# A graph network's first edge stage: selection matrices as the weights, edge values as the moving operand, and one product that adds two halves and turns them

## The reference, cut to what matters

```python
h = jnp.maximum(_layernorm(x, axis=-1), 0.0)
r = edge_index[1]                                   # dst, sorted
c1ij = jnp.concatenate([h[r], edge_attr_64], axis=1)
e = jax.nn.softplus(c1ij @ W1 + b1)                 # 128 values per edge
e = jax.nn.softplus(e @ W2 + b2)                    # 128 values per edge
out = e @ W3 + b3
agg = jax.ops.segment_sum(out, r, num_segments=12500)
x = x + h + agg
```

## Time and profile before

| what | value |
|---|---|
| median of 3 runs | 7407.81 us (7402.51 to 7408.39) |
| the profiled execution, its own time | 7408.24 us |
| its span (first to last instruction) | 7406.7 us |
| mean granted TensorE clock | 0.874 |
| PE busy over the span | 6552.2 us, 88% |
| DVE, POOL, ACT busy | 5031.9 us, 4983.3 us, 3071.1 us |
| the first edge stage, first to last `mm1` | 111.4 us to 1419.9 us |

### The profile page before, as it was taken

One profiled execution on the slowest core, in us unless ns is written; L12 is line 12 of the kernel. 1 busy time (PEld: TensorE's weight loads), 2 busy tenths in 40 slices (PEclk: granted clock), 3 DMA queues, 4 the chain that ended last, 5 costly groups with the idle time before them and its releaser, 6 DMA issues.

```text
span 7406.7 us, 164037 instructions
## 1 busy us (share of the span) xinstructions
PE 6552.2 (88%) x35087; PEld 3274.1 (44%) x35087; DVE 5031.9 (68%) x15478; ACT 3071.1 (41%) x4956; POOL 4983.3 (67%) x6107
## 2 busy tenths in 40 slices
PE   6999999966787777777869999999999989998998
PEld 4666666532333333333324444444444434443443
DVE  7777777657888888888856777777777743332232
ACT  4777777634555555555523333333333300000000
POOL 4544544347777777777757777777777657765776
PEclk9999999975656565666579999999999999998999
DMA  4333333242232323232322222222222266665775
GB/s 129 107 106 106 106 107 105 95 144 83 86 90 85 90 85 90 85 90 85 91 53 60 61 63 61 61 61 62 62 61 61 50 177 189 189 187 170 199 200 165
DMA packets 774396, 770.05 MB, mean 104 GB/s; under 512 B 242791, under 2 KB 585891, under 8 KB 774179
## 3 DMA queue, kind: packets, MB, share of 16 engines
q1 hardware_dynamic: 575923, 589.45, 25.5%
q0 software_dynamic: 147776, 160.99, 10.6%
q10 hardware_dynamic: 50544, 17.90, 1.0%
HBM read 581.31 MB, written 187.29 MB: 104 GB/s over the span
## 4 chain that ended last, share of the span: by engine, by line
PE 59%; POOL 18%; issue 9%; DVE 8%; SPq 3%; DMA 1%; ACT 1%; DVEq 1%; POOLq 0%; ACTq 0%
POOL zone L1051 15%; PE ps L2566 9%; PE ps L2406 9%; PE ps L2211 6%; PE ps L2193 5%; PE ps L2218 5%; PE ps L2571 4%; PE ps L2398 4%; POOL zone L1090 2%; PE ps L2425 2%; PE ps L2209 2%; PE ps L2391 2%; PE ps L2387 2%; PE ps L2416 1%; DVE zone L1368 1%
## 5 line engine op out<-in xcount | busy, mean ns | idle before, releaser
L1051 POOL DMA_INDIRECT zone<-tab_msg,zone x1664 | 1636.3, 983 | 520.0 <-issue 512.1
L1051 POOL DMA_INDIRECT zone<-tab_u,src_i x1664 | 1604.7, 964 | 562.2 <-issue 552.2
L1368 DVE TENSOR_TENSOR zone<-ps,zone 128x512 f32<-128x512 f32 x1664 | 1068.0, 686 | 452.4 <-PE ps L2398 332.8
L2020 ACT ACTIVATE zone<-ps 128x792 fp8e4<-128x792 f32 x1200 | 966.7, 829 | 881.0 <-PE ps L2370 861.8
L2370 PE MATMUL ps<-zone 128*128 128x396 bf16 x2400 | 933.5, 478 | 290.8 <-DVE zone L1654 156.2
L2193 PE MATMUL ps<-zone 128*128 128x64 f32 (+1 forms) x6656 | 831.2, 282 | 174.9 <-DMA zone<-tab_msg,zone 158.6
L1654 DVE TENSOR_SCALAR zone<-tT,zone 128x392 bf16<-128x392 f16 x2400 | 968.5, 404 | 0.0
L2406 PE MATMUL ps<-zone,w_bas 128*64 128x512 f32 x3328 | 900.0, 619 | 0.0
L2193 PEld LDWEIGHTS ps<-zone 128*128 128x128 f32 (+1 forms) x6656 | 754.1, 196 | 320.0 <-issue 272.9
L2566 PE MATMUL ps<-zone 128*128 128x512 fp8e4 x3332 | 845.1, 383 | 26.6 <-DMA zone<-adj 16.2
L1333 DVE SCALAR_TENSOR_TENSOR zone<-zone,ps 128x512 f32<-128x512 f32 x832 | 566.3, 686 | 274.9 <-ACT zone L1921 174.5
(11 more groups left out here) (320 smaller groups left out, 8792.8 us busy)
## 6 DMA issues: line engine op xcount, KB each, us to landing
zone<-adj SPq DMA_DIRECT2D x238, 768.0 KB
adj<-zone SPq DMA_DIRECT2D x150, 784.0 KB, 3.4
zone<-in_dst_row SPq DMA_DIRECT2D x832, 128.0 KB, 2.7
zone<-in_ea_T SPq DMA_DIRECT2D x416, 128.0 KB, 2.6
zone<-src_lin SPq DMA_DIRECT2D x2448, 0.5 KB
zone<-adj SPq DMA_DIRECT2D x34, 896.0 KB
tab_msg<-zone SPq DMA_DIRECT2D x104, 256.0 KB, 2.3
zone<-tab_msg,zone POOLq DMA_INDIRECT x1664
```

What stands on the lines that cost most here:

```text
L1051: nc.gpsimd.indirect_dma_start(out=gat(e, u)[:, k, :], out_offset=None, in_=table, in_offset=bass.IndirectOffsetOnAxis(ap=numbers[:, c * T ...
L1368: nc.vector.tensor_tensor(zed[:, b % SL, :], bank(2 + b % 2), inter[:, u % 2, b % 2, :], ALU.mult) \
L2020: nc.scalar.activation(staging[m][:, :, at_ * 2 * WN:(at_ + 1) * 2 * WN].rearrange("p b (w d) -> p w b d", w=2), pair_[:, :, 0:CX].rearran ...
```

## The change

The sum is made in two steps. First (`sum_rows_of`), the selection of each group is the weights (128 edges x 64 nodes) and `hid2` is the moving operand (128 columns). Groups 0 and 2 write to partitions 0 to 63 of a bank, groups 1 and 3 to partitions 64 to 127. The result is 64 nodes on the partitions, twice, with 128 values along the row. Two chunks share bank 4 or 5. Second, ACT copies the two chunks of a bank to SBUF in one instruction (`move_rows`, into `sum_rows`), and PE multiplies each with `two_eyes`, two identity matrices of 64 one above the other (`turn_rows`): this adds the two halves and turns the result back into 128 values x 64 nodes, in bank 6 or 7, from where DVE adds it to `acc` as before. DVE's addition moves from lag 7 to lag 9.

```diff
+        two_eyes = sb("two_eyes", [P128, D])
+        sum_rows = spare.rearrange("p (v s c) -> p v s c", v=2, s=2)
+            const(nc.gpsimd.tensor_tensor(two_eyes[:, :], ident[:, 0:D], ident[:, D:P128], ALU.add))
...
-            ADD_LAG = {0: 7, 1: 4, 2: 7}
+            ADD_LAG = {0: 9, 1: 4, 2: 7}
...
-                    dve.wait_ge(agg_done, done(ga, it, u, depth(e)))
+                    dve.wait_ge(rows_summed if e == 0 else agg_done, done(ga, it, u, depth(e)))
...
-                        (5, soft(hid2_ready, softened2, agg_done, soft2, hid2, 2)),
+                        (5, soft(hid2_ready, softened2, rows_summed, soft2, hid2, 2)),
                         (0, selT_stage(0, p, slice(D, P128), 3)),
                         (4, sel_stage(0, p)),
-                        (ADD_LAG[0], add_stage(0, p, H, (4, 5, 6, 7)))]
+                        (ADD_LAG[0], add_stage(0, p, H, (6, 7)))]
...
-                chunk_loop(act, [(2, soften(mm1_done, hid1_ready, softened1, soft1, 0)), (4, soften(mm2_done, hid2_ready, softened2, soft2, 2))])
+                def move_rows(it, u, _):
+                    if u % 2 == 0:
+                        return
+                    v = u // 2
+                    act.wait_ge(rows_summed, done(g, it, u))
+                    act.wait_ge(agg_done, done(g, it, u, 4))
+                    nc.scalar.activation(sum_rows[:, v % 2], bank(4 + v % 2)[:, 0:2 * P128].rearrange("p (s c) -> p s c", s=2), ACT.Copy) \
+                        .then_inc(rows_moved, 1)
+
+                chunk_loop(act, [(2, soften(mm1_done, hid1_ready, softened1, soft1, 0)), (6, move_rows),
+                                 (4, soften(mm2_done, hid2_ready, softened2, soft2, 2))])
...
-                chunk_loop(pe, [
-                    (1, mm1), (3, mm2),
-                    (5, sum_stage(0, p, H, lambda u: hid2[:, u % 2, :].rearrange("p (k c) -> p k c", k=TL),
-                                  hid2_here, (4, 5, 6, 7)))])
+                gv = pe.snap(p * PAIRS)
+
+                def sum_rows_of(it, u, _):
+                    v = u // 2
+                    pe.wait_ge(hid2_ready, done(g, it, u))
+                    pe.wait_ge(sel_built, done(g, it, u))
+                    pe.wait_ge(rows_moved, done2(gv, it, v, 2))
+                    for k in range(TL):
+                        last = mm(bank(4 + v % 2)[half(k), u % 2 * P128:(u % 2 + 1) * P128], sel(0, u)[:, k, :],
+                                  hid2[:, u % 2, k * P128:(k + 1) * P128], start=k < 2, stop=k >= TL - 2)
+                    last.then_inc(rows_summed, 1)
+
+                def turn_rows(it, u, _):
+                    v = u // 2
+                    pe.wait_ge(rows_moved, done2(gv, it, v))
+                    pe.wait_ge(agg_added, done(g, it, u, 2))
+                    mm(bank(6 + u % 2)[:, 0:W], sum_rows[:, v % 2, u % 2, :], two_eyes[:, :], start=True, stop=True) \
+                        .then_inc(agg_done, 1)
+
+                chunk_loop(pe, [(1, mm1), (3, mm2), (5, sum_rows_of), (8, turn_rows)])
```

More of the change, by code:

```diff
@@ L439, in build_gnn @@
         hid2_ready = sem("hid2_ready")
+        rows_summed = sem("rows_summed")
+        rows_moved = sem("rows_moved")
         sums_weighed = sem("sums_weighed")
@@ L690, in build_gnn @@
         ALL_LOADED = 16 * (len(LOADS) + 1)
-        N_CONSTS = 25
+        N_CONSTS = 26
         N_LATE = 3
@@ L1859, in _ @@
             for s_, n in ((softened1, 2 * RING), (softened2, 2 * RING), (inter_moved, RP),
-                          (tanh_done, RP), (tan_ready, RP), (moved_out, 2)):
+                          (tanh_done, RP), (tan_ready, RP), (moved_out, 2), (rows_moved, RP)):
                 act.sem_inc(s_, n)
@@ L2129, in _ @@
         def _(pe):
-            for s_, n in ((agg_done, RING), (mm1_done, RING), (mm2_done, RING),
+            for s_, n in ((agg_done, RING), (rows_summed, RING), (mm1_done, RING), (mm2_done, RING),
                           (inter_done, RP), (bas_spread, NBAS * RP), (weighed, NBAS * RP), (tan_turned, RP),
```

## The result

The changed kernel takes 7486.6 us (median of 4 runs, 7484.75 to 7493.57), the kernel before in the same session 7408.1 us. The ratio is 1.011, with a 95% interval of 1.0097 to 1.0122. The forecast was 7514 us. The difference of the spans is 7485.6 - 7406.7 = 78.9 us.

What follows compares the result with a forecast made beforehand. PE alone was taken to bound the first edge stage: 7408.24 + 75 (416 steps, each 0.18 us longer) + 28 (DVE's read) + 3 (stage end) = 7514 us; own range 7495 to 7535, 8 in 10 7465 to 7545.

Steps and rivals of the forecast that it cites:

- What bounds the stage, and the form of the argument: First edge stage: bound by PE alone, so each 0.1 us per step on PE is 42 us of the kernel.
- The halves run at once: New sum on PE: products for the two array halves run in pairs, 0.60 us to the next group's start.
- The change of form: PE, into and out of the new sum: changing the tiling empties the array, 0.10 us for each change.
- The turn: `turn_rows` on PE: two records of 0.11 us plus 0.10 for exposed first weights, 0.32 us per step.
- the rival in which it is hidden: Turn on PE: its weights load during the drain, 0.1 us less per step, about 7477 us; chance 0.10.
- DVE's read of positions: Every eighth step, behind the addition's wait on DVE: read becomes visible for 0.57 us, some 50 times, +28 us.
- the rival in which the read stays hidden: DVE, every eighth step: the read can start before the addition's wait, 7486 us; chance 0.18.
- ACT: ACT's added copy, 0.384 us per pair of chunks, and its wait: hidden, costed at nothing.
- The end of the stage: After the last sum: copy and turns about 1 us, the last addition's own read 1.85 us; +3 us.
- The rival of a faster kernel: PE in the first edge stage: changes of form are hidden, step 2.99 us, 7386 us; chance 0.06.

Runs made afterwards that it cites:

- experiment 2: Changed kernel with the four products of the new sum in the order 0, 2, 1, 3; 7495.5 us in one run.
- experiment 3: Kernel before the change, with the bias product of `mm2` on 128 rows (125 of them zeros) instead of 3; 7285.5 us, ratio 0.9833.
- experiment 5: Changed kernel with DVE's addition at lag 10 and the turn as two products of 64 columns of weights instead of one of 128; 7411.7 us, ratio 1.0006.
- experiment 1: Changed kernel with DVE's addition at lag 10 instead of 9; 7465.0 us, ratio 1.0075.
- experiment 4: Changed kernel with ACT's copy of two chunks made twice, once into an unused place; 7497.7 us, ratio 1.0118.
- experiment 6: Changed kernel with DVE's lag 10, the turn as two products of 64 columns of weights, and the bias on 128 rows; 7287.5 us, ratio 0.9836.
- experiment 8: Changed kernel with two-product turn, 128-row bias, DVE's lag 11, and sums and turns of two chunks made together every second step; 7244.2 us, ratio 0.9775.

## Why the prediction came out as it did

- **What bounds the stage, and the form of the argument**: right. The stage is PE's starts, and the whole difference lies between 113 and 1511 us.
- **The halves run at once**: right in size, 0.59 us for the interpolated 0.60; the eight records start in four pairs, 0.007 us apart. By experiment 2 the pairs form in the other order of the products too.
- **The change of form**: right in kind, confirmed for rows by experiment 3 and for columns by experiment 5; 0.09 on entry for 0.10. The runs price the gap; that it is the time in which the array empties, as the prediction has it, none of them shows.
- **The turn**: this is the term that was mis-sized, 0.32 forecast, 0.27 measured. I added 0.10 for exposed weights to two full records of 0.11. The 0.10 came from groups with 128 moving columns, where the first record's own moving time is as long as a load. With 64 columns the second record starts only 0.16 us after the first, and `mm1` 0.11 us after that. By the prediction's own 0.053 us for 64 moving columns, the 0.16 are an exposed load of 0.11 and that moving time. So the load is exposed as forecast, the rival in which it is hidden (7477 us) is out, and the first record was 0.05 too dear. That the second load runs beside the first product is argued from the spacing, not shown by a run. With the 0.01 each of entry and sum, the step is +0.11 instead of +0.18, 28 us of the kernel. That is the miss from 7514; the other terms are off by 2 us or less each and nearly cancel.
- **DVE's read of positions**: right in place, cause and size: 0.61 us per loop turn for 0.57, and experiment 1 takes it away. The long step took 3.84 us for the 3.9 of the sum, and 0.05 more came in the next. This must be said because the rival in which the read stays hidden gave 7486 us, which is the measured time to the microsecond. It is right by accident. Whoever reads only the total would pick the wrong story; the idle row before L2233 tells them apart.
- **ACT**: hidden, as costed, by experiment 4.
- **The end of the stage**: 1.6 us for 3, and 2 us at its beginning that I had at nothing. I took 1.85 us for the last addition's own read, but that one reads a single position and took 0.32 us:

```profile
L515 DVEq TENSOR_LOAD <-base_i x1: 317/317/317, 1509.6 to 1509.6; - x1
```

- **The rival of a faster kernel** failed because both changes are paid. Its half of truth is shown by experiments 6 and 8: with the turn in the same form the swap is level, and once the changes are shared as well, it wins. The Trainium skill (TensorEngine Tiling (Array Packing), Performance Considerations) advises the swap with column tiling for a moving dimension of 64. The runs agree with it where the tiled products of two chunks stand together (41 us faster in experiment 8 than in experiment 3), and not where one such group stands alone among products of the full array (1.1% slower with a turn in the full form, level in experiments 5 and 6).

## What to carry to other kernels

Price a product on PE by the spacing of starts, including what stands next to it: the bias of 3 rows cost 0.30 us in gaps and exposed weights, more than the 0.22 us that the same product takes with 128 rows. Group products of one form, or pad the odd one with zeros to the full form; here the padding alone gave 1.7%. And when a lag is moved on an in-order engine, look at what stands behind the new wait that isn't computation, such as a read into registers every eighth step. Last, don't let the total choose the story: two mechanisms of this prediction differed by 28 us, and the wrong one had the right number.

## What the runs showed of the hardware that I had not expected

- A bf16 product of 3 rows between float32 products of 128 rows makes a step 0.30 us longer than the same product on 128 rows, 125 of them zeros: about 0.10 us before it, after it, and in the first weights behind it.
- Records of products with 64 columns of weights start in pairs even if the order in the program has two products for the same half next to each other (0.013 us apart instead of 0.007). Which two make a pair the trace doesn't show.
- Reading eight numbers into registers takes 1.84 us on DVE, and on POOL and SP, in the trace of the same kernel, 0.57 and 0.53 us:

```profile
L515 SPq TENSOR_LOAD <-base_i x45: 521/527/531, 201.7 to 1380.5; - x45
...
L515 POOLq TENSOR_LOAD <-base_i x44: 572/576/584, 223.9 to 1375.9; - x44
```

- On DVE the time of such a read goes with how many numbers it reads: 0.32 us for the one at the end of the changed kernel's stage, 1.63 for the seven at the end of the stage before the change, 1.84 for eight. That is about 0.22 us for each number more.
